# Causal attention on one core: queries and keys as two fp32 words in two 64-row halves of the array, instead of three bf16 parts in one

## The reference

```python
xn = layernorm(x)
q, k, v = (xn @ W.T split in 16 heads of 16, for W in (Wq, Wk, Wv)); q, k = rope(q), rope(k)
scores = where(causal, q @ k.T / sqrt(16), finfo.min)
attention = (softmax(scores) @ v) @ Wo.T
ffn = fp4_linear(silu(fp4_linear(xn, w_gate)) * fp4_linear(xn, w_up), w_down)   # inner size 704
out = x + attention + ffn
```

## Time and profile before

| what | value |
|---|---|
| time, median of 3 runs | 2565.34 us (2563.74 to 2568.26) |
| span of the profiled execution | 2561.9 us |
| own time of the profiled execution | not given apart; its span is 3.4 us below the median |
| TensorE busy | 2440.4 us (95%) |
| DVE busy | 2236.7 us (87%) |
| ScalarE busy | 1594.3 us (62%) |
| GpSimd busy | 166.3 us (6%) |
| mean granted TensorE clock | 0.979 |

### The profile page before, as it was taken

The page is one execution under the profiler, slowest core; times in us unless marked ns, Lnnn a source line. Parts: engine busy times, 40 slices in busy tenths (PEclk is TensorE's granted clock), DMA queues, the critical chain, the costliest instruction groups (busy, mean ns, idle before and its releaser), DMA issues. The chain is left out here.

```text
span 2561.9 us, 51480 instructions
## 1 busy us (share of the span) xinstructions
PE 2440.4 (95%) x14338; PEld 1170.2 (46%) x14338; DVE 2236.7 (87%) x4841; ACT 1594.3 (62%) x3260; POOL 166.3 (6%) x466
## 2 busy tenths in 40 slices
PE   5999999999996999999999999999999999999987
PEld 3555555555564234434444344344344344443335
DVE  8999999999996989898899899889888888998834
ACT  3545554554552277777777777777777777777740
POOL 2001101101101000000000000000000000000010
PEclk8999999999998699999999999999999999999999
DMA  6212112122123412212112122122122121120034
GB/s 199 74 56 67 64 64 69 56 70 71 54 72 90 113 35 61 70 33 67 43 54 73 31 62 67 35 62 74 35 61 69 33 68 41 55 61 6 20 125 173
DMA packets 141411, 168.57 MB, mean 66 GB/s; under 512 B 14048, under 2 KB 107536, under 8 KB 141200
## 3 DMA queue, kind: packets, MB, share of 16 engines
q1 hardware_dynamic: 137856, 159.49, 19.9%
q10 hardware_dynamic: 3344, 6.41, 0.7%
HBM read 97.17 MB, written 67.90 MB: 64 GB/s over the span
## 5 line engine op out<-in xcount | busy, mean ns | idle before, releaser
L1247 ACT ACTIVATE prob<-score 128x512 f32<-128x512 f32 (+3 forms) x2560 | 1158.6, 542 | 390.2 <-PE score L1178 192.1
L1322 DVE TENSOR_REDUCE top<-tile 128x1 f32<-128x512 f32 x1536 | 956.8, 680 | 104.0 <-PE tile L1153 95.7
L1178 PE MATMUL score<-qs,ks 99*128 99x512 bf16 (+3 forms) x2560 | 812.6, 350 | 7.8 <-ACT prob L1247 3.1
L1153 PE MATMUL tile<-ks,qs 96*128 96x512 bf16 (+3 forms) x2560 | 778.0, 355 | 25.7 <-DMA ks<-qkp 16.5
L1198 PE MATMUL acc<-prob,vs 128*32 128x512 f32 (+3 forms) x5120 | 535.3, 536 | 0.0
L1327 DVE CUSTOM_DVE_ANT_0 tile<-tile,mask 128x128 f32<-128x128 f32 (+3 forms) x1024 | 469.5, 518 | 61.5 <-PE tile L1153 59.3
L1178 PEld LDWEIGHTS score<-qs,ks 99*128 99x128 bf16 x2560 | 244.6, 97 | 414.5 <-ACT prob L1247 225.6
L1153 PEld LDWEIGHTS tile<-ks,qs 96*128 96x128 bf16 x2560 | 239.0, 98 | 298.0 <-DVE top L1322 84.6
L349 PE MATMUL gu<-wguT,xT 128*128 128x512 f32 (+1 forms) x768 | 310.7, 557 | 0.0
L1198 PEld LDWEIGHTS acc<-prob,vs 128*32 128x32 f32 x5120 | 133.9, 109 | 244.1 <-issue 138.9
L1183 PE MATMUL score<-identb,maskb 128*128 128x128 bf16 x1024 | 212.2, 220 | 0.0
(11 more groups left out here) (130 smaller groups left out, 1723.0 us busy)
## 6 DMA issues: line engine op xcount, KB each, us to landing
qkp<-parts SPq DMA_DIRECT2D x192, 128.0 KB
vscr<-vt SPq DMA_DIRECT2D x16, 1024.0 KB, 5.4
vs<-vscr SPq DMA_DIRECT2D x16, 1024.0 KB, 6.1
oscr<-acc_sb SPq DMA_DIRECT2D x64, 256.0 KB, 2.1
qs<-qkp SPq DMA_DIRECT2D x64, 192.0 KB, 3.4
ks<-qkp SPq DMA_DIRECT2D x64, 192.0 KB, 3.3
x_all<-in_x SPq DMA_DIRECT2D x16, 512.0 KB, 9.0
qs<-qkp SPq DMA_DIRECT2D x64, 128.0 KB, 3.1
```

What stands on the lines that cost most here:

```text
L1153: mm = nc.tensor.matmul(bank[:, h * width:(h + 1) * width], qs[par][0:ROWS, h0 + h, q0:q0 + P], ks[par][0:ROWS, h0 + h, k0:k0 + width], st ...
L1178: mm = nc.tensor.matmul(bank[:, 0:width], ks[par][0:ROWS_M, h, kb * P:(kb + 1) * P], qs[par][0:ROWS_M, h, qb * GROUP + off:(qb + 1) * GROU ...
L1247: nc.scalar.activation(prob[:, k % PROB_SLOTS, 0:width], score[:, k % SCORE_SLOTS, 0:width], ACT.Exp, scale=HEAD ** -0.5).then_inc(probs_r ...
L1322: nc.vector.tensor_reduce(top[:, j, h0, c:c + 1], bank, AX.X, ALU.max).then_inc(tile_taken, 1)
```

## The change

Queries and keys are split in two fp32 words: DVE keeps the upper bits of `raw` with a bitwise and (12 low bits cleared) and subtracts for the rest; ScalarE's two casts and DVE's third part go. A head then has 48 rows (three products of words times 16) plus 3 rows for the maximum, and two heads lie one above the other, from partitions 0 and 64, in buffers of the same size as before. Their products are issued as float32r from these halves, so heads 0 and 2 use rows 0 to 63 of the array and heads 1 and 3 rows 64 to 127. Masks are now added on TensorE for tiles and scores, each as two bf16 products of 64 columns a head over the 64 rows of the same half, and all reductions on DVE are plain. Diagonal tiles of 128 and 256 columns now hold two heads each (12 diagonal reductions for a block of queries). Loads take four DMAs for three, and stores eight of 256 KB for twelve of 128 KB. `ORDER` is new: weigh steps (w) have letters of their own and stand alone (39 separate blocks), the copy of the sums stands at a. 82 tile events are done ahead. Half the rows of ones are set by DVE before the first keys are loaded. The reciprocal sums are kept in another buffer.

The diff, cut to its core:

```diff
-TERMS = PARTS * (PARTS + 1) // 2
-ROWS = TERMS * HEAD
+SPLITS = 2
+HIGH_BITS = -(1 << 12)
+ROWS = SPLITS * (SPLITS + 1) // 2 * HEAD
 ROWS_M = ROWS + PARTS
+SIDE = 64
+SIDES = P // SIDE
+LOADS = SPLITS * SIDES
+CUT_COLS = 4 * P + 2 * SIDE
...
-LEAD = 0.52
-ONE_PAIR = float(np.array([0x3F803F80], np.uint32).view(np.float32)[0])
-WEIGH_AT, WEIGH_STEPS = 3, 2
-ORDER = ("stssttsststtssttsstsssstsststsststsssrtststststststostssstststssttststststsststssttsstststssstss"
-         "sttstsststssssttsstttsstststsossssttsstttsststsssstsststttssttssssstststsststtssssstsrtstsststts"
-         "tsssstsststsststrssssttssstottstsstsssststtststststststssstststssttsttsstssstssttssrtststsssstss"
-         "tststtsttsstssssttsttsstsstsssststssttssttstssstssstttsstsso")
+AHEAD = 80
+ORDER = ("sssttssttsssttssssttswtssssttsstwsttstswssrtststtwaststtswssttstwstststwsttssttststswtsssttwssst"
+         "tttssswtststswssttstswtaststtswsttstswtsttsswttsstswsttsttsswsststtwtstsstwtssttsrststtstswtttss"
+         "swssttstsststststsswsststwstststwststtssratsttsstwtsttsswtsststwssstttwsswsttstswtsttsswstststwt"
+         "ssttswtsstsrtstststwtststswtssswtssttststtssstwttssstwssstttwwta")
...
-                nc.scalar.copy(parts[:, 0, :, :], raw[:]).then_inc(part1_ready, 1)
...
-                nc.scalar.copy(parts[:, 1, :, :], turned[:]).then_inc(part2_ready, 1)
...
-            def second_rest(g):
+            def high_part(g):
+
+                dve.wait_ge(rope_ready, g + 2)
+                dve.wait_ge(parts_stored, g * (SPLITS * 4 * 16) + 1)
+                nc.vector.tensor_scalar(parts[:, 0, :, :].bitcast(I32), raw[:].bitcast(I32), HIGH_BITS, None,
+                                        ALU.bitwise_and).then_inc(part1_ready, 1)
+
+            def low_part(g):
 
                 dve.wait_ge(part1_ready, g + 1)
-                nc.vector.tensor_tensor(turned[:], raw[:], parts[:, 0, :, :], ALU.subtract).then_inc(rest_ready, 1)
-
-            def third_part(g):
-
-                dve.wait_ge(part2_ready, g + 1)
-                nc.vector.tensor_tensor(parts[:, 2, :, :], turned[:], parts[:, 1, :, :],
-                                        ALU.subtract).then_inc(part3_ready, 1)
+                nc.vector.tensor_tensor(parts[:, 1, :, :], raw[:], parts[:, 0, :, :],
+                                        ALU.subtract).then_inc(raw_free, 1)
...
                 scale_h(g, 0)
+                high_part(g)
                 round_h(g, more, 0)
                 scale_h(g, 1)
                 scale_h(g, 2)
                 round_h(g, more, 1)
                 round_h(g, more, 2, lambda: add_down(g, more, 0))
                 scale_h(g, 3)
-                second_rest(g)
+                low_part(g)
...
-            heads = (4, 2, 1, 1)[j]
-            for h in range(0, HG, heads):
+            heads = (2, 2, 1, 1)[j]
+            for h in range(HG // heads):
...
+    first = tiles.index(next(e for e in tiles if e[0] == "tile" and e[1] == AHEAD))
...
+        elif letter == "w":
+            plan.append(weighs[weighed])
+            weighed += 1
+        elif letter == "a":
+            plan += [("take", outs), ("out", outs)]
...
-                for parts in range(PARTS, 0, -1):
-                    first = (PARTS - parts) * HEAD if which else 0
-                    sp.dma_start(buf[row:row + parts * HEAD, :, c * GROUP:(c + 1) * GROUP],
-                                 src[first:first + parts * HEAD]).then_inc(loaded, 16)
+                for parts in range(SPLITS, 0, -1):
+                    first = (SPLITS - parts) * HEAD if which else 0
+                    for side in range(SIDES):
+                        sp.dma_start(buf[side * SIDE + row:side * SIDE + row + parts * HEAD, :, c * GROUP:(c + 1) * GROUP],
+                                     src[first:first + parts * HEAD, side::SIDES, :]).then_inc(loaded, 16)
...
+                if c == 0:
+                    sp.wait_ge(ones_ready[it], SIDES)
...
+            def stacked(buf, h, rows, first, width):
+
+                side = h % SIDES * SIDE
+                return buf[side:side + rows, h // SIDES, first:first + width].bitcast(F32R)
+
+            def mask_half(bank, h, of, half, heads, width, first):
+
+                side = h % SIDES * SIDE
+                sides = slice(side, side + SIDE)
+                out = bank[:, 0:heads * width].rearrange("p (h c) -> p h c", h=heads)[:, :, first:first + SIDE]
+                eye = cutb[sides, 4 * P:4 * P + heads * SIDE].rearrange("p (h c) -> p h c", h=heads)
+                at = (of * 2 + half) * P
+                return nc.tensor.matmul(out, cutb[sides, at:at + P], eye, start=False, stop=True, skip_group_check=True)
...
+                                          stacked(qs[par], h0 + h * SIDES, ROWS, q0, P),
+                                          stacked(ks[par], h0 + h * SIDES, ROWS, k0, width),
                                           start=(h == 0), stop=True, skip_group_check=True)
+                if c == qb:
+                    for half in range(2):
+                        mm = mask_half(bank, h0, 1, half, heads, width, width - P + half * SIDE)
...
-                mm = nc.tensor.matmul(bank[:, 0:width], ks[par][0:ROWS_M, h, kb * P:(kb + 1) * P],
-                                      qs[par][0:ROWS_M, h, qb * GROUP + off:(qb + 1) * GROUP],
-                                      start=True, stop=True)
+                mm = nc.tensor.matmul(bank[:, 0:width], stacked(ks[par], h, ROWS_M, kb * P, P),
+                                      stacked(qs[par], h, ROWS_M, qb * GROUP + off, width), start=True, stop=True)
                 if j is not None:
 
-                    mm = nc.tensor.matmul(bank[:, 0:P], maskb[:], identb[:], start=False, stop=True,
-                                          skip_group_check=True)
+                    for half in range(2):
+                        mm = mask_half(bank, h, 0, half, 1, width, half * SIDE)
...
+            for side in range(0, P, SIDE):
+                nc.gpsimd.memset(ks[1][side + SIDE // 2:side + SIDE, :, :].rearrange("p h c -> p (h c)"), 1.0
+                                 ).then_inc(ones_ready[1], 1)
...
+            for side in range(0, P, SIDE):
+                nc.vector.memset(ks[0][side + SIDE // 2:side + SIDE, :, :].rearrange("p h c -> p (h c)"), 1.0
+                                 ).then_inc(ones_ready[0], 1)
...
-                if c < qb:
-                    nc.vector.tensor_reduce(top[:, j, h0, c:c + 1], bank, AX.X, ALU.max).then_inc(tile_taken, 1)
-                    return
-                dve.sem_inc(dve_passed, 1)
-                for h in range(heads):
-                    head = bank[:, h * width:(h + 1) * width]
-                    last = nc.vector.tensor_tensor_reduce(
-                        out=head, in0=head, in1=mask[:, GROUP - width:GROUP],
-                        scale=1.0, scalar=MASK, op0=ALU.add, op1=ALU.max, accum_out=top[:, j, h0 + h, c:c + 1])
-                last.then_inc(tile_taken, 1)
+                nc.vector.tensor_reduce(top[:, j, h0:h0 + SIDES * (heads - 1) + 1:SIDES, c:c + 1],
+                                        bank[:, 0:heads * width].rearrange("p (h c) -> p h c", h=heads),
+                                        AX.X, ALU.max).then_inc(tile_taken, 1)
...
-    d["qkp"] = nc.dram_tensor("qkp", [2, HGS, GROUPS, PARTS * HEAD, HG, GROUP], BF16).ap()
+    d["qkp"] = nc.dram_tensor("qkp", [2, HGS, GROUPS, SPLITS * HEAD, HG, GROUP], F32).ap()
```

More of the change, by code:

```diff
@@ L834, in attention_plan @@
         tiles.append(("top", qb))
[L836 to L845 removed]
+    first = tiles.index(next(e for e in tiles if e[0] == "tile" and e[1] == AHEAD))
     events = [(*t, 0) for t in tiles[first:]] + [(*t, 1) for t in tiles[:first]]
     steps = [(qb, kb, kb - 4 * qb if kb >= 4 * qb else None) for qb in range(QB) for kb in range(4 * qb + 4)]
[L850 to L859 removed]
+    scores = [("scores", HG * n + h, n, *step) for n, step in enumerate(steps) for h in range(HG)]
+    weighs = [("weigh", n, *step) for n, step in enumerate(steps)]
+    plan, rows, outs, scored, weighed, at = [], [], 0, 0, 0, 0
     for letter in ORDER:
@@ L875, in attention_plan @@
                 at += 1
-    assert scored == len(scores) and at == len(events) and outs == QB and not rows
+    assert scored == len(scores) and weighed == len(steps) and at == len(events) and outs == QB and not rows
     for qb in range(QB):
@@ L1259, in iteration @@
                         exponentials(it, e)
-                    elif e[0] == "weigh" and e[1] == last_step[e[2]]:
-                        take_acc(it, e)
+                    elif e[0] == "take":
+                        take_acc(it, e[1])
             for it in range(ITERS):
```

108 lines of the change are left out of this document (39 added, 69 removed).

## The result

The changed kernel takes 2502.61 us (median of four runs, 2494.85 to 2506.07), against 2565.8 us for the kernel before beside it: a ratio of 0.9742, 95% interval 0.9722 to 0.9763. That is 63 us faster where the forecast had 151; 2502.6 lies in the range, but in the part that was kept for the rivals.

A forecast was written before the change was run, and what follows sets the result against it. TensorE was taken to bound attention (95.2 of 99.7 us an iteration), DVE close behind. Savings of 30 + 5 - 4 + 108 + 12 = 151 us from 2565 gave 2414 us, range 2335 to 2580.

The forecast's parts named there:

- clock granted in full: TensorE in attention: one pass at 2.4 GHz, 0.417 ns a column, 0.22 us for a 512-column bf16 product.
- Out projection: unchanged: Output projection after attention: the change was taken to neither gain nor lose time there.
- The period at full clock: Attention iteration, one value load to the next: 92.5 us taken from 89 to 97, against 99.7 before.
- the upper bound: TensorE's iteration in attention if weight loads don't overlap: 46 us replaces 41, up to 92 in all instead of 80.
- float32r at bf16's price: Score and tile products in attention: a float32r product of 512 columns takes the bf16 value, 0.22 us.
- ScalarE's waits: Attention: ScalarE's 1.19 us idle after eight exps, put down to paired weigh steps, goes with single steps.
- First block: Block before attention: DVE's path shrinks by 1.2 to 2.4 us a group; 2.0 x 15 = 30 us taken.
- The 5 us at the block's end: First block's end: without the third part, last stores start some 3 us earlier and issue is halved; 5 us saved.
- Entry: Start of attention: keys issued 4.3 to 8.5 us after queries, waiting for DVE's two memsets; 5 us lost.
- No concurrency: Rival: row halves don't run side by side in attention; TensorE's period 108 us, 2670 us in all; chance 0.12.
- the slow type: Rival: float32r takes two passes in attention, period 120 us, 2860 in all; four passes far worse; chance 0.07.
- Loads and switches eat it: Rival: non-overlapping weight loads and dearer mode changes give a 100 us attention period, 2534 us in all; chance 0.09.

The follow-up runs named there:

- e1: Changed kernel with all query-key products and masks issued on rows 0 to 63 only: 4548.02 us.
- e4: Changed kernel with its single weigh steps joined in pairs again, 20 blocks instead of 39: 2730.61 us, ratio 1.0635 to the kernel before.
- e14: Changed kernel with 12 unused bf16 products added per iteration, ahead of the first query block's narrow scores: 2461.79 us.
- e15: As e14, with the second half's ones of the first key buffer set by GpSimd: 2456.59 us, ratio 0.9577 to the kernel before.
- e12: Changed kernel with all 224 mask products of an iteration left out, so the diagonal is not causal: 2490.11 us.
- e3: Changed kernel with tiles and scores reading only the upper 16 bits of each word as bf16: 2386.81 us.

## Why the prediction was right and wrong

**The step that failed: one pass at 2.4 GHz with the "clock granted in full".** The forecast read that off for the kernel before and priced every product of the changed one by it; whether the changed work would keep the clock it never asked. At 0.43 us for each us at half clock this covers nearly all of the shortfall from the first score to the last weigh:

- 13 iterations: 13 x 8.7 x 0.43 = 49 of 46.7 us.
- Iteration 0, from the first score (864.6, before 874.8) to its value load: 108.9 us where the kernel before took 106.6 and 7.2 less were forecast, 9.5 short; 27.0 us at half clock instead of 5.3 are worth 9.3. The lead ahead of it (44.9 us, before 45.8) is at half clock in both kernels, and took 1 us less, as forecast.
- From the last value load to the last weigh: 28.2 against 3.4 us at half clock, 10.7 of 9.2 us.

**The end: a hidden queue, which the forecast put at nothing ("Out projection: unchanged").** The 6.5 us behind the last weigh are SP's. Its 38.5 us between the last two stores had been just hidden before; in every run but e1 and e4, whose last weigh comes too late for it, these stores stand 38.4 to 38.7 us apart, and the copied sums wait. The clock costs nothing there: from the last store to the end it is 88.0 us, 88.3 before, though 20.5 us from the last weigh on are at half clock and 13.7 were before. No run moved SP's loads.

Shown by intervention: e14 and e15 added work, at one place, and got 41 and 46 us; e12 took work away and got 12 of the 40 or so that its period at full clock promised. Shown by this is that the clock's falls cost the time and that work at an iteration's beginning decides on them. What it is in the changed work that makes the clock fall stays open.

**The period at full clock: right, 92.4 against 92.5**, though half by luck: the working for the upper bound gives 80 - 41 + 46 = 85 us with loads and not 92, and the 92.5 was a choice between bounds. DVE was forecast at 85 us and has 85.8; a mode change 0.24 and measured 0.25; row halves overlap, as taken. *float32r at bf16's price* failed in part: in a stream it is true (0.235 against 0.228 us), behind masks and at the first product of a run it is not, and e3 prices it at 5.1 us an iteration. The forecast had loads only in its upper bound ("if the loads don't overlap each other").

**ScalarE's waits: wrong.** They were to go with the pairs of weigh steps. For scores over 1000 us it waits 102 + 97 us where it waited 121 + 116 before, the longest now 2.2 us.

**First block: mis-sized, 1.05 us a group instead of 2.0.** The and did fill ScalarE's wait; the third part's removal uncovered the next one, 1.03 us, which the forecast should have named as what is late next. The 5 us at the block's end were 2: the queries wait for DVE's last add (799.24), not for the last stores (791.78 to 795.0).

**Entry: keys 8.8 us after the queries instead of 4.3 to 8.5**, just beyond my bounds: 0.91 us ahead of each of the two memsets came on top of 2 x 3.47. The first tile is 6.1 us later against the queries than before, where 5 were charged.

**Rivals.** No concurrency and the slow type are refuted by the six products in 0.93 us and by e1. "Loads and switches eat it" had the right term (loads that show) at the wrong size: 5.1 us of an iteration, not 7 beyond TensorE's 92.

## What to carry to other kernels

Once a change makes TensorE's instructions narrower or fewer, price it at both clock levels: look in the trace of before for where narrow products stand together, and forecast an iteration at either clock. Where iterations with the same instructions differ in length, plot their length against the time at half clock; the line's start is the period you argued for, and a dozen well-placed products may buy the rest. And when work that covers another engine is removed, name what that cover was over: twice here (third part, statistics) the next wait opened at once, and at the end a shorter attention uncovered SP's queue.

## What the runs showed of the hardware that I had not expected

- Less work can be slower and more work faster: 24 products added, 16 us faster; 12 added, 41; the same 24 elsewhere, 65 slower; 224 removed, 12 faster only.
- A loss in packing came with a larger one in clock: 39 more same-half neighbours cost 6.8 us of TensorE's time and put 50 us of each iteration at 1.2 GHz, where it had been 8.7; with all on one half TensorE was busy all the time and never got back to 2.4 GHz (clock 0.50 for 2953 us).
- A float32r product of 512 columns takes one pass, 0.235 us (bf16 0.228), and its weight load 0.19 us, twice bf16's; it is hidden behind 512 columns and not behind 64 (0.316 us against 0.229).
- DVE's memset of 32 x 4096 takes 3.47 us beside GpSimd's (7.07 for two).
- With TensorE recorded busy without a gap and the same instructions, one iteration of the changed kernel keeps 2.4 GHz and the next loses it.
